# Message instructions of four steps instead of two in the first graph's edge pass

## The chip, the cores and the metric

One core of a Trainium2 chip runs the whole program. The metric is the time of one execution on the device in microseconds (us). Engines are named as in the profile: PE is TensorE (the matrix engine), PEld its weight loads, DVE is VectorE, ACT is ScalarE, POOL is GpSimd, SP is SyncE. A wait is a semaphore wait in an engine's own instruction stream: everything behind it on that engine waits too.

## The reference

Two rounds of a graph layer and a feed-forward layer on 6250 nodes of 256 features, with 106250 edges sorted by their destination. Only the attention over the edges of the first graph layer matters here:

```python
Q = (h @ Wq).reshape(n, H, HD)          # n = 6250, H = 8 heads, HD = 32
K = (h @ Wk).reshape(n, H, HD)
V = (h @ Wv).reshape(n, H, HD)
score = jnp.einsum('ehd,ehd->eh', K[src], Q[dst]) / np.sqrt(HD) + edge_bias
m = jax.ops.segment_max(score, dst, num_segments=n)
ex = jnp.exp(score - m[dst])
denom = jax.ops.segment_sum(ex, dst, num_segments=n)
attn = ex / denom[dst]
out = jax.ops.segment_sum(attn[:, :, None] * V[src], dst, num_segments=n)
```

After it come the projection, layer norms, a feed-forward layer, a feed-forward layer on the top half of the nodes, a second graph layer and a mixture of eight experts. All is float32.

## The kernel before

`attend_edges` works through the edges in steps of 128 edges, one edge per partition. A step belongs to one block of 128 destination nodes. 16 steps make a chunk (`CH`), 4 a quarter (`QU`), 2 a pair, and there are 55 chunks (`CHUNKS_OF`), 880 steps. A step goes through these stations:

- POOL gathers the key and value rows of its 128 source nodes into `ring`, 44 steps deep (L411).
- PE multiplies a one-hot matrix with the block's queries, so that each edge has its query row (`query`, L436, two steps into one bank), and DVE multiplies these with the keys (`product`, L661, 512 columns) and sums over each head (`dot`, L667, four steps).
- Per chunk DVE makes the scores (`score_of`, L674), PE transposes them (L457), and a row of scans on DVE finds each edge's segment maximum (L681 to L731), with two small detours through PE: `row` (L461 to L463), which `before` (L691) waits for, and `ends` (L467, L468), which `carry_of` (L716) waits for. ACT takes the exponential, PE transposes it back and ACT copies it into `prob` (L595).
- DVE multiplies the values with the weights into `msg` (`messages`, L753), 264 columns a step of which 32 of each 33 are messages and the 33rd is the weight itself, copied in by ACT (`denominators`, L580). `msg` has two halves of one quarter each. ACT also makes the one-hot matrices `sel` of each quarter (`one_hot`, L571 and L574).
- PE multiplies `sel` with `msg` (`add_up`, L450, into one of two banks), and DVE adds the result to the block's row in `qa` (`add`, L766). `add_up` of step i waits for the addition of step i - 2, since it has two banks; `add` of step i waits for that matmul.

Three chunks are in work at once: in a turn, c is the chunk whose products are made, a the one whose maxima are found, b the one whose messages are made and added up. The order of the instructions of a turn is written out by hand, on DVE in `turn` (L777 to L829), on PE and ACT in functions of the same name. `score_of` opens the turn on DVE. PE's order, as far as it matters here, is: transposed scores, add_up 0 and 1, a query pair and a one-hot, `row`, add_up 2 and 3, a query pair, `ends`, add_up 4, and so on to add_up 12 and 13, a query pair and one-hot of the next chunk, add_up 14, another query pair, add_up 15.

Before the change a message instruction makes one pair, 512 columns, and adds 1 to `s_msg`. PE waits for `s_msg` at every even step, for the pair of that step alone; at the first step of a quarter it also waits for the one-hot (`s_rs`) and for the denominators (`s_den`). A pair that opens a quarter waits until PE has added up the quarter two before it. ACT overwrites a half of `prob` when all messages of the chunk two back are made.

Of the kernel before, what the change touches and what calls it, by code (L numbers as in the profile page):

```python
# [16 lines left out]
ALU = mybir.AluOpType  # L17
# [3 lines left out]
P = 128  # L21
# [308 lines left out]
def attend_edges(nc, g, qa):  # L330
# [3 lines left out]
    with Phase(nc, "attend") as m:  # L334
# [81 lines left out]
        def _(pe):  # L416
# [23 lines left out]
            def add_up(b, *steps):  # L440
                for u in steps:
                    q, i = u // QU, b * CH + u
                    if u % QU == 0:
                        pe.wait_ge(s_rs, b * quarters + q + 1)
                        pe.wait_ge(s_den, b * quarters + q + 1)
                    if u % 2 == 0:
                        pe.wait_ge(s_msg, i // 2 + 1)
                    if i >= SUM_BANKS:
                        pe.wait_ge(s_add, i - SUM_BANKS + 1)
                    nc.tensor.matmul(ps_agg[i % SUM_BANKS][:, 0:AGG], sel[:, q % 2, u % QU, :], msg[:, q % 2, u % QU, :],  # L450
                                     start=True, stop=True).then_inc(s_agg, 1)
# [105 lines left out]
        def _(act):  # L557
# [33 lines left out]
            def weights_of(a):  # L591
                act.wait_ge(s_prob, a + 1)
                if a >= 2:
                    act.wait_ge(s_msg, (a - 1) * CH // 2)
# [44 lines left out]
        def _(v):  # L639
# [107 lines left out]
            def messages(b, pair):  # L747
                q, first, u = pair // 2, (b * CH + pair * 2) % RING1, pair * 2
                if pair == 0:
                    v.wait_ge(s_weights, b + 1)  # L750
                if pair % 2 == 0 and b * quarters + q >= 2:
                    v.wait_ge(s_agg, (b * quarters + q - 1) * QU)
                nc.vector.tensor_tensor(msg[:, q % 2, u % QU:u % QU + 2].rearrange("p u (h c) -> p u h c", c=HC)[:, :, :, 0:HD],  # L753
                                        ring[:, first:first + 2, D:2 * D].rearrange("p u (h d) -> p u h d", h=H),
                                        prob[:, b % 2].rearrange("p h u -> p u h")[:, u:u + 2, :].unsqueeze(3)
                                        .to_broadcast([P, 2, H, HD]), ALU.mult).then_inc(s_msg, 1)
# [20 lines left out]
            def turn(c, a, b):  # L777
# [8 lines left out]
                of(b, messages, 1)  # L786
# [6 lines left out]
                of(a, top_of)  # L793
                of(b, add, at, 2)
                of(a, drop_of)
                of(b, messages, 2)
# [4 lines left out]
                of(b, messages, 3)  # L801
# [10 lines left out]
                of(b, messages, 4)  # L812
# [4 lines left out]
                of(b, messages, 5)  # L817
# [4 lines left out]
                of(b, messages, 6)  # L822
# [3 lines left out]
                of(b, messages, 7)  # L826
# [2139 lines left out]
```

## Time and profile before

| | us |
|---|---|
| median of 3 runs | 5128.81 |
| lowest and highest | 5120.07, 5130.25 |
| the profiled execution | 5127.6 |
| its span, first to last instruction | 5125.8 |

| engine | busy us | share of the span |
|---|---|---|
| PE | 3909.5 | 76% |
| DVE | 3118.7 | 61% |
| POOL | 2344.6 | 46% |
| ACT | 1867.0 | 36% |

The pass of the change is the first of three long DVE stretches; its message instructions run from 284.5 to 1740.5 us of the span. A row of the profile gives a group of instructions by its line in the kernel, its engine and its tiles: busy us and the mean ns of one, then the engine's idle time just before them and who ended it. In a timeline the rows stand in order of time: start, duration, engine, line, count of merged instructions, and idle time before the first with its releaser. A step of `add_up` is two matmul instructions, so "x2" is one step and "x4" two. DVE durations overlap a little: the next one starts before the last has ended. PEclk is the clock that TensorE was granted, as a share of 2.4 GHz.

### The profile page before, as it was taken

To read this page: it belongs to the slowest core of one execution; us is meant where nothing else is said; L and a number is where in the kernel's file an instruction comes from. 1 tells how busy PE (TensorE), PEld (TensorE's weight loads), DVE (VectorE), ACT (ScalarE), POOL (GpSimd) and SP (SyncE) were. 2 spreads that over 40 slices of the span, in tenths; PEclk is the share of its full clock that TensorE was granted. 3 is DMA by queue.
4 is the path that set the end of the run, shared out by engine and by line. 5 is a ranking of instruction groups with operands and counts; after the bars stand their busy time and mean duration, and the time that the engine had idled before them with its cause. 6 is when DMAs were issued, how large, how long until landed. Compare 5 with 4: busy or idle time off the path is not lost. (4 is left out here: it accounts for less than half of the span.)

```text
span 5125.8 us, 69922 instructions
## 1 busy us (share of the span) xinstructions
PE 3909.5 (76%) x16154; PEld 2806.8 (55%) x16282; DVE 3118.7 (61%) x7733; ACT 1867.0 (36%) x5097; POOL 2344.6 (46%) x2387
## 2 busy tenths in 40 slices
PE   6977777777777659967965777777774349999998
PEld 3555555555555448856843444444443336777776
DVE  3389989999999766662045777777777761111111
ACT  1334444444444213311213555555553303333332
POOL 2265555556555340001045777777773402333332
PEclk8989999999999789987966778787776569999999
DMA  2565555555555232211064444444443441211111
GB/s 75 182 186 160 164 159 160 161 160 165 162 156 160 66 105 92 92 58 41 31 201 129 110 109 110 108 111 110 111 110 86 132 148 29 33 31 31 31 32 27
DMA packets 316121, 553.59 MB, mean 108 GB/s; under 512 B 63430, under 2 KB 213782, under 8 KB 315856
## 3 DMA queue, kind: packets, MB, share of 16 engines
q0 software_dynamic: 137120, 388.63, 28.9%
q1 hardware_dynamic: 178736, 161.98, 10.4%
q8 instruction: 99, 1.62, 0.1%
q14 instruction: 166, 1.36, 0.1%
HBM read 459.75 MB, written 90.62 MB: 107 GB/s over the span
## 5 line engine op out<-in xcount | busy, mean ns | idle before, releaser
L411 POOL DMA_INDIRECT attend_ring<-kv_rows,all_step_src x880 | 867.5, 986 | 592.5 <-PE attend_ps_agg L450 440.0
L914 POOL DMA_INDIRECT edge_ring<-head_rows,all_step_src x880 | 863.9, 982 | 285.2 <-issue 185.5
L950 PE MATMUL edge_ps_agg<-edge_msg,edge_sel 128*128 128x264 f32 x1760 | 644.7, 492 | 208.3 <-DVE graph_acc L1249 105.7
L450 PE MATMUL attend_ps_agg<-attend_msg,attend_sel 128*128 128x264 f32 x1760 | 591.3, 441 | 243.5 <-DVE graph_qa L766 138.1
L2799 DVE TENSOR_TENSOR moe_gl<-moe_ps_h,moe_act 128x341 f32<-128x341 f32 x210 | 107.9, 514 | 776.7 <-PE moe_ps_h L2717 776.7
L950 PEld LDWEIGHTS edge_ps_agg<-edge_msg,edge_sel 128*128 128x128 f32 x1760 | 374.9, 237 | 352.6 <-issue 171.3
L450 PEld LDWEIGHTS attend_ps_agg<-attend_msg,attend_sel 128*128 128x128 f32 x1760 | 317.7, 204 | 415.3 <-DVE graph_qa L766 182.7
L436 PE MATMUL attend_ps_q<-graph_qa,attend_sel_t 128*128 x1760 | 512.2, 419 | 7.1 <-DVE attend_prod L661 6.4
L2717 PE MATMUL moe_ps_h<-experts_w,moe_xt 128*128 x1680 | 501.8, 451 | 0.6 <-ACT moe_xt L2748 0.6
L766 DVE SCALAR_TENSOR_TENSOR graph_qa<-graph_qa,all_step_same,attend_ps_agg 128x264 f32 x880 | 421.8, 479 | 58.8 <-PE attend_ps_agg L450 42.4
L571 ACT ACTIVATE attend_sel<-all_lane,all_step_dst 128x128 f32<-128x128 f32 x880 | 281.2, 390 | 429.6 <-PE attend_ps_agg L450 414.0
L2671 POOL DMA_INDIRECT out<-moe_y,moe_to_row x105 | 166.6, 1587 | 579.9 <-ACT moe_y L2757 565.0
L436 PEld LDWEIGHTS attend_ps_q<-graph_qa,attend_sel_t 128*128 128x128 f32 x1760 | 368.6, 212 | 76.0 <-issue 11.0
L2717 PEld LDWEIGHTS moe_ps_h<-experts_w,moe_xt 128*128 128x128 f32 x1680 | 311.1, 190 | 146.5 <-issue 3.1
L1249 DVE TENSOR_TENSOR graph_acc<-graph_acc,edge_ps_agg 128x264 f32 x880 | 365.7, 416 | 30.6 <-PE edge_ps_agg L950 20.1
L1237 DVE TENSOR_TENSOR edge_msg<-edge_ring,edge_prob 128x256 f32<-128x256 f32 x880 | 345.8, 414 | 37.0 <-ACT edge_prob L1113 35.1
L1061 ACT ACTIVATE edge_sel<-all_lane,all_step_dst 128x128 f32<-128x128 f32 x880 | 279.5, 389 | 237.4 <-PE edge_ps_agg L950 237.4
L2702 PE MATMUL moe_ps_y<-experts_w,moe_gt 128*128 x1260 | 309.9, 387 | 0.7 <-ACT moe_gt L2774 0.7
L661 DVE TENSOR_TENSOR attend_prod<-attend_ps_q,attend_ring 128x512 f32<-128x512 f32 x440 | 297.8, 678 | 20.3 <-DMA attend_ring<-kv_rows,all_step_src 10.1
L753 DVE TENSOR_TENSOR attend_msg<-attend_ring,attend_prob 128x512 f32<-128x512 f32 x440 | 298.9, 679 | 0.3 <-issue 0.2
L1808 PE MATMUL ffn_ps_h<-ffn_xt,ffn_wa 128*128 128x256 f32 x1216 | 272.0, 382 | 11.5 <-ACT ffn_xt L1831 11.5
L1850 ACT ACTIVATE ffn_ht<-ffn_ps_h,ffn_ba 128x256 f32<-128x256 f32 x304 | 144.2, 474 | 363.9 <-PE ffn_ps_h L1808 363.9
(423 smaller groups left out, 6374.8 us busy)
## 6 DMA issues: line engine op xcount, KB each, us to landing
attend_ring<-kv_rows,all_step_src POOLq DMA_INDIRECT x880
edge_ring<-head_rows,all_step_src POOLq DMA_INDIRECT x880
kv_rows<-qkv_kv SPq DMA_DIRECT2D x25, 512.0 KB, 2.9
experts_w<-in_w_t SPq DMA_DIRECT2D x16, 682.0 KB
attend_mask<-run_starts SPq DMA_DIRECT2D x440, 8.1 KB
edge_mask<-run_starts SPq DMA_DIRECT2D x440, 8.1 KB
head_rows<-hds_hh SPq DMA_DIRECT2D x25, 264.0 KB, 3.4
qkv_x<-in_x SPq DMA_DIRECT2D x25, 256.0 KB, 3.3
```

The source lines that it names most:

```text
L411: nc.gpsimd.indirect_dma_start(ring[:, step % RING1, :], None, g.kv_rows, bass.IndirectOffsetOnAxis(g.step_src[:, step:step + 1], 0)).then ...
L436: ins = nc.tensor.matmul(ps_q[k % QBANKS][:, i, :], sel_t[:, q % 2, u % QU, :], queries[:, bass.ds(blocks[u % U], 1), :].rearrange("p b d ...
L450: nc.tensor.matmul(ps_agg[i % SUM_BANKS][:, 0:AGG], sel[:, q % 2, u % QU, :], msg[:, q % 2, u % QU, :], start=True, stop=True).then_inc(s_ ...
L661: nc.vector.tensor_tensor(prod[:, at:at + 2, :], ps_q[k % QBANKS][:], ring[:, first:first + 2, 0:D], ALU.mult).then_inc(s_prod, 1)
L753: nc.vector.tensor_tensor(msg[:, q % 2, u % QU:u % QU + 2].rearrange("p u (h c) -> p u h c", c=HC)[:, :, :, 0:HD], ring[:, first:first + 2 ...
L766: nc.vector.scalar_tensor_tensor(at[u % U], at[u % U], g.step_same[:, i:i + 1], ps_agg[i % SUM_BANKS][:, 0:AGG], ALU.mult, ALU.add).then_i ...
L914: nc.gpsimd.indirect_dma_start(ring[:, n % slots, u, :], None, g.head_rows, bass.IndirectOffsetOnAxis(g.step_src[:, step:step + 1], 0)).th ...
L950: nc.tensor.matmul(ps_agg[i % BANKS][:, 0:AGG], sel[:, q % 2, u % QU, :], msg[:, q % 2, u % QU, :], start=True, stop=True).then_inc(s_agg, 1)
L1237: nc.vector.tensor_tensor(msg[:, q % 2, u % QU].rearrange("p (h c) -> p h c", c=HC)[:, :, 0:HD], ring[:, b % slots, u, 0:D].rearrange("p ( ...
L1249: nc.vector.tensor_tensor(at[u % U], at[u % U], ps_agg[i % BANKS][:, 0:AGG], ALU.add).then_inc(s_add, 1)
L2702: last = nc.tensor.matmul(ps_y[:], gt[0:size, c, :], w2[0:size, :, c, :][:, bass.ds(e, 1), :].rearrange("p a d -> p (a d)"), start=(c == 0 ...
L2717: last = nc.tensor.matmul(ps_h[2 * i + hf][:, 0:EHALF], xt[:, slot, k, :], w13[:, :, k, i, hf * EHALF:(hf + 1) * EHALF][:, bass.ds(e, 1), ...
```

## The change

`messages` makes a whole quarter in one instruction of 1024 columns, four in a chunk, and adds 1 to `s_msg` for each. In DVE's order the four stand where pairs 0 and 4 stood (quarters 0 and 2), between the top row and the addition of step 2 (quarter 1), and where pair 6 stood (quarter 3). PE waits at every step for the quarter of that step. Every quarter's instruction waits for the release of its half of `msg`. ACT's wait counts quarters instead of pairs.

```diff
@@ -443,8 +443,7 @@
                     if u % QU == 0:
                         pe.wait_ge(s_rs, b * quarters + q + 1)
                         pe.wait_ge(s_den, b * quarters + q + 1)
-                    if u % 2 == 0:
-                        pe.wait_ge(s_msg, i // 2 + 1)
+                        pe.wait_ge(s_msg, b * quarters + q + 1)
                     if i >= SUM_BANKS:
                         pe.wait_ge(s_add, i - SUM_BANKS + 1)
                     nc.tensor.matmul(ps_agg[i % SUM_BANKS][:, 0:AGG], sel[:, q % 2, u % QU, :], msg[:, q % 2, u % QU, :],
@@ -591,7 +590,7 @@
             def weights_of(a):
                 act.wait_ge(s_prob, a + 1)
                 if a >= 2:
-                    act.wait_ge(s_msg, (a - 1) * CH // 2)
+                    act.wait_ge(s_msg, (a - 1) * quarters)
                 nc.scalar.activation(prob[:, a % 2].rearrange("p h u -> p (h u)"), prob_e, ACT.Copy).then_inc(s_weights, 1)
 
             for s in range(2):
@@ -744,16 +743,16 @@
                 nc.vector.scalar_tensor_tensor(heads_at, shrinks.unsqueeze(2).to_broadcast([P, H, HC]), 1.0, heads_at,
                                                ALU.add, ALU.mult).then_inc(s_v, 1)
 
-            def messages(b, pair):
-                q, first, u = pair // 2, (b * CH + pair * 2) % RING1, pair * 2
-                if pair == 0:
+            def messages(b, q):
+                first, u = (b * CH + q * QU) % RING1, q * QU
+                if q == 0:
                     v.wait_ge(s_weights, b + 1)
-                if pair % 2 == 0 and b * quarters + q >= 2:
+                if b * quarters + q >= 2:
                     v.wait_ge(s_agg, (b * quarters + q - 1) * QU)
-                nc.vector.tensor_tensor(msg[:, q % 2, u % QU:u % QU + 2].rearrange("p u (h c) -> p u h c", c=HC)[:, :, :, 0:HD],
-                                        ring[:, first:first + 2, D:2 * D].rearrange("p u (h d) -> p u h d", h=H),
-                                        prob[:, b % 2].rearrange("p h u -> p u h")[:, u:u + 2, :].unsqueeze(3)
-                                        .to_broadcast([P, 2, H, HD]), ALU.mult).then_inc(s_msg, 1)
+                nc.vector.tensor_tensor(msg[:, q % 2].rearrange("p u (h c) -> p u h c", c=HC)[:, :, :, 0:HD],
+                                        ring[:, first:first + QU, D:2 * D].rearrange("p u (h d) -> p u h d", h=H),
+                                        prob[:, b % 2].rearrange("p h u -> p u h")[:, u:u + QU, :].unsqueeze(3)
+                                        .to_broadcast([P, QU, H, HD]), ALU.mult).then_inc(s_msg, 1)
 
             def add(b, at, *steps):
                 for u in steps:
@@ -783,7 +782,6 @@
                 of(c, product, 1)
                 of(a, heads_of)
                 of(b, rescale, at[0])
-                of(b, messages, 1)
                 of(b, add, at, 0)
                 of(a, before)
                 of(a, row_forward)
@@ -791,14 +789,13 @@
                 of(a, row_backward)
                 of(b, add, at, 1)
                 of(a, top_of)
+                of(b, messages, 1)
                 of(b, add, at, 2)
                 of(a, drop_of)
-                of(b, messages, 2)
                 of(a, after)
                 of(b, add, at, 3)
                 of(c, product, 2)
                 of(a, carry_of)
-                of(b, messages, 3)
                 of(a, forward)
                 of(b, add, at, 4)
                 of(c, product, 3)
@@ -809,21 +806,19 @@
                 of(b, add, at, 6)
                 of(a, shrink_of)
                 of(c, product, 4)
-                of(b, messages, 4)
+                of(b, messages, 2)
                 of(b, add, at, 7)
                 of(c, product, 5)
                 at = rows_of(b, 1) if b is not None else [None] * U
                 of(b, add, at, 8)
-                of(b, messages, 5)
                 of(c, dot, 2)
                 of(b, add, at, 9)
                 of(c, product, 6)
                 of(b, add, at, 10)
-                of(b, messages, 6)
+                of(b, messages, 3)
                 of(b, add, at, 11)
                 of(c, product, 7)
                 of(b, add, at, 12)
-                of(b, messages, 7)
                 of(b, add, at, 13)
                 of(c, dot, 3)
                 of(b, add, at, 14, 15)
```

## Rows read from the trace of the kernel before

**Rows 1.** Busy time: window, its length, PE, PEld, DVE, ACT, POOL, PEclk, DMA, GB/s.

```profile
300.00:1700.00 1400.00, 1053.69 (x4170) 762.75 (x4239) 1284.15 (x2672) 580.64 (x1625) 821.00 (x832) 0.93 0.57 160
954.26:979.53 25.27, 18.49 (x80) 13.12 (x81) 24.33 (x51) 11.08 (x32) 16.12 (x17) 1.00 0.60 171
1006.05:1032.36 26.31, 19.82 (x79) 14.48 (x81) 24.63 (x52) 11.08 (x32) 15.84 (x17) 0.94 0.58 164
1032.36:1060.56 28.20, 21.37 (x80) 15.31 (x81) 24.41 (x52) 11.07 (x32) 15.64 (x17) 0.88 0.54 152
1060.56:1088.36 27.80, 21.47 (x80) 15.63 (x81) 24.78 (x52) 11.07 (x32) 16.29 (x17) 0.88 0.58 160
```

**Rows 2.** Groups of instructions on VectorE, from 300 to 1700 us.

```profile
L753 DVE TENSOR_TENSOR attend_msg<-attend_ring,attend_prob 128x512 f32<-128x512 f32 x420 | 285.3, 679 | 0.1
...
L667 DVE TENSOR_REDUCE attend_dots<-attend_prod 128x32 f32<-128x1024 f32 x211 | 253.9, 1203 | 0.0
```

**Rows 3.** All score instructions (L674): shortest, median, longest ns, first and last start.

```profile
L674 DVE SCALAR_TENSOR_TENSOR attend_score<-attend_dots,all_step_bias x55: 373/375/381, 264.9 to 1702.5; 128x128 f32<-128x128 f32 x55
```

**Rows 4.** Waits from 300 to 1700 us: total us, times, the longest.

```profile
PE attend_ps_agg L450 <- DVE graph_qa L766: 135.5, 108, 2.1
...
PE attend_ps_agg L450 <- DVE attend_msg L753: 58.4, 54, 1.1
...
PE attend_ps_agg L450 <- ACT attend_msg L580: 29.7, 52, 0.6
```

**Rows 5.** The page's costliest groups: messages of the second graph's pass.

```profile
L1237 DVE TENSOR_TENSOR edge_msg<-edge_ring,edge_prob 128x256 f32<-128x256 f32 x880 | 345.8, 414 | 37.0 <-ACT edge_prob L1113 35.1
```

**Rows 6.** Timeline of VectorE in the chunk from 954.26 to 979.53.

```profile
954.48 0.67 DVE L753 TENSOR_TENSOR attend_msg<-attend_ring,attend_prob 128x512 f32<-128x512 f32 x1
955.07 0.69 DVE L661 TENSOR_TENSOR attend_prod<-attend_ps_q,attend_ring 128x512 f32<-128x512 f32 x1
...
958.38 0.16 DVE L691 COPY attend_ps_tp<-attend_so_far 1x8 f32<-1x8 f32 x1
958.57 0.41 DVE L695 TENSOR_TENSOR_SCAN attend_c_in<-attend_keep,attend_ps_tp 1x128 f32<-1x128 f32 x1
...
968.43 0.67 DVE L753 TENSOR_TENSOR attend_msg<-attend_ring,attend_prob 128x512 f32<-128x512 f32 x1
...
970.59 0.68 DVE L753 TENSOR_TENSOR attend_msg<-attend_ring,attend_prob 128x512 f32<-128x512 f32 x1
...
973.71 0.68 DVE L753 TENSOR_TENSOR attend_msg<-attend_ring,attend_prob 128x512 f32<-128x512 f32 x1
...
975.48 0.49 DVE L766 SCALAR_TENSOR_TENSOR graph_qa<-graph_qa,all_step_same,attend_ps_agg 128x264 f32 x1
975.89 0.69 DVE L753 TENSOR_TENSOR attend_msg<-attend_ring,attend_prob 128x512 f32<-128x512 f32 x1
...
978.79 0.49 DVE L766 SCALAR_TENSOR_TENSOR graph_qa<-graph_qa,all_step_same,attend_ps_agg 128x264 f32 x1 [0.30 <-PE attend_ps_agg L450]
```

**Rows 7.** Timeline of TensorE in the same chunk.

```profile
955.60 1.13 PE L450 MATMUL attend_ps_agg<-attend_msg,attend_sel 128*128 128x264 f32 x4 [0.58 <-ACT attend_msg L580]
...
958.07 0.27 PE L463 MATMUL attend_ps_tp<-all_ident,attend_runs 128*1 128x128 f32 x1
...
969.35 1.13 PE L450 MATMUL attend_ps_agg<-attend_msg,attend_sel 128*128 128x264 f32 x4
...
972.85 0.71 PE L450 MATMUL attend_ps_agg<-attend_msg,attend_sel 128*128 128x264 f32 x2 [0.81 <-DVE graph_qa L766]
...
974.65 1.13 PE L450 MATMUL attend_ps_agg<-attend_msg,attend_sel 128*128 128x264 f32 x4 [1.08 <-DVE attend_msg L753]
...
976.70 0.64 PE L450 MATMUL attend_ps_agg<-attend_msg,attend_sel 128*128 128x264 f32 x2
...
978.04 0.61 PE L450 MATMUL attend_ps_agg<-attend_msg,attend_sel 128*128 128x264 f32 x2
```

**Rows 8.** Timeline of ScalarE in the same chunk.

```profile
955.25 0.40 ACT L580 ACTIVATE attend_msg<-attend_prob 128x32 f32<-128x32 f32 x2
```

## The prediction

> **What bounds the kernel now.** The change touches only the attention pass over the edges of the first graph, so I read only that stretch. First the busy time of its steady part: VectorE (DVE) works 1284 of 1400 us, 92%, TensorE (PE) 1054 us, 75% [rows 1]. VectorE is the engine nearest its limit, and the message instructions are a large item on it: 420 of 679 ns in that stretch, eight to a chunk [rows 2]. The pass has 55 chunks of 16 steps; their score instructions start 26.62 us apart on average ((1702.5 - 264.9) / 54) [rows 3].
>
> Then who waits for whom. TensorE waits for VectorE's additions 108 times (135.5 us) and for the messages 54 times (58.4 us, up to 1.1), and 52 times, 0.57 us each, for ScalarE's denominators [rows 4]. That is about once per chunk at fixed places, so the loop is not VectorE alone: it is VectorE and TensorE handing work to each other, and the places must be looked at one by one.
>
> Last, one chunk in order of time: the one from 954.26 to 979.53, whose TensorE clock was 1.00 (2.4 GHz) all through, so that nothing but the waits sets its 25.27 us [rows 1]. The other chunks shown take 26.31 to 28.20 at a mean granted clock of 0.94 to 0.88. Steps of a chunk are numbered 0 to 15, pairs 0 to 7, quarters 0 to 3.
>
> **The price of the new instruction.** 256 columns take 414 ns in the second graph's pass [rows 5], 512 take 679 [rows 2]: 1.035 ns a column. 1024 columns then take 1.21 us; the reduction that reads 1024 columns takes 1.203 [rows 2]. VectorE starts the next instruction before the last has ended: pair 0 starts at 954.48, its follower at 955.07, 0.59 later [rows 6]. With 0.53 for 512 more columns the new one holds the engine 1.13. Two old ones hold it 1.20: a quarter saves 0.07 us, 220 quarters 15 us. If the new one took as long as two (1.36 us) nothing would be saved; I take 1.21, the nearer rows.
>
> The Trainium skill ("VectorE: DVE Perf Modes", the section on the fixed extra latency of SBUF-source operations) charges each fp32 tensor_tensor (N + 151) / 0.96 ns. Its durations agree with the 679 above; read as time of the engine it would save 157 ns a quarter, 35 us in all. The 0.59 us from start to start speaks against that reading.
>
> **Quarter 0, start of the chunk.** TensorE's step 0 starts at 955.60 [rows 7]. Its messages (pair 0) ended at 955.15; the last thing it waited for was the denominators, the first of two ScalarE copies from 955.25, which end at 955.50 and 955.65 [rows 8]. With one instruction for four steps the messages end at 954.48 + 1.21 = 955.69 and take the place of that wait. How long from there to the matmul? Step 12 is released by pair 6, which ends at 974.39, and starts at 974.65: 0.26. So step 0 starts at 955.95, **0.35 later**. What is queued behind it on TensorE is steps 0 and 1, a query pair, a one-hot and the row transposes, back to back until 958.34; VectorE's L691 waits for these and starts at 958.38 [rows 6, 7]. It goes to 958.73. VectorE has pair 1's 0.60 fewer and quarter 0's 0.53 more before it, so it arrives early and stands idle: its saving ends there.
>
> **Quarter 1.** It moves from before step 0's addition (and pair 2 and 3 from after the drop and the carry) to the place after the top row. From L691 to the second dot product two pairs of 0.60 go and one of 1.13 comes, -0.07; small dependent instructions that the pairs covered are bare now, 0.19 each as from L691 to L695 [rows 6]; the gap of the top row is covered instead. I put the sum at -0.03. Step 4 has its messages long before. The shift is **0.32**. In chunks at the low clock VectorE waits for the carries of TensorE there instead, which carry the same 0.35.
>
> **Quarter 2.** Pair 4 started at 968.43 and ended at 969.10; step 8 started at 969.35 [rows 6, 7]. The new one ends at 968.43 + 0.32 + 1.21 = 969.96, step 8 starts at 970.21, 0.86 later, and a query pair and steps 9 and 10 are queued behind. But TensorE stood idle 0.81 before step 11, at 972.85, for step 9's addition [rows 7]. That slack takes it: the addition comes by VectorE's own shift, 0.32 + 1.13 - 2 x 0.60 = **0.25**, since pair 5 (970.59) is gone too.
>
> **Quarter 3.** It starts at 973.71 + 0.25 = 973.96 and ends at 975.17, where pair 6 ended at 974.39. TensorE stood idle 1.08 for exactly this [rows 7]. With the same 0.26, step 12 starts at 975.43, **0.78 later** than 974.65. Behind it are steps 12 and 13, the next chunk's first queries, step 14, more queries and step 15, without a wait to 978.04. Pair 7 (975.89) ended at 976.58, when TensorE was just ready for step 14, at 976.70: its removal frees nothing on TensorE. On VectorE it frees 0.60, after step 12's addition (975.48, now 976.26), but the addition of step 15, which stood idle 0.30 for TensorE and started at 978.79, then only waits longer [rows 6, 7]. The next score follows it. So the chunk ends 0.77 later.
>
> **Nothing else is on the path.** The extra semaphore wait at every odd step is passed before the wait for the addition that follows it, in TensorE's queue, hidden by the matmuls still running: at 0; bare, it could cost no more than the 0.12 us between release and matmul at step 14. ScalarE waits only for chunks two back. The gathers on the GpSimd queue are released by the same steps, a little later, with POOL busy 821 of 1400 us. SyncE's row loads are released by the same scores. Nothing of them is moved. On VectorE quarters 2 and 3 wait for the half of the buffer that steps 0 to 3 and 4 to 7 used; both stand behind additions of later steps, so these waits are met.
>
> **Sum.** 54 chunk periods x 0.77 = 41.6 us. The granted clock adds a little: 26.62 less 25.27 is 1.35 us a chunk, and if the low stretches keep their share of a period 3% longer, 2 us more. The profiled execution took 5127.6 us (span 5125.8), 1.2 under the median of the three runs, 5128.8: with 42 to 44 added to either, 5171.
>
> Bounds. If TensorE starts 0.12 behind its messages, as at step 14 (976.58 and 976.70), both waits are 0.14 shorter: 0.49 a chunk, 5155. If the instruction takes 1.36: about 0.15 more a chunk, 5179.
>
> **The rivals.**
> A. VectorE is the bound after all: for it, 92%; against it, the 1.08 and 0.30 of idle time at the chunk's end. It decides if TensorE reaches step 12 later than the messages even when these take 1.21. Then the kernel gains 15 us, 5114; and if the engine's time falls by the difference of durations, 2 x 0.679 - 1.21 = 0.15 a quarter, 33 us, 5096. Chance 0.09.
> B. Gain and waits cancel, the same time within 0.2% (10 us, about what a measurement of this kernel can tell from no change): 0.11.
> C. Only quarter 3 costs: TensorE makes up the 0.35 before L691 (a step 0 released by the denominators as before). 0.42 a chunk, 23 us, 5151: 0.15.
> D. The waits are as forecast and TensorE's clock falls more often. Low stretches are there already: a chunk whose mean granted clock is 0.94 costs 1.04 more than one at 1.00, one at 0.88 2.5 to 2.9 more [rows 1]. TensorE's idle time grows by 0.35 at the start of a chunk and 0.5 before step 12. One more low stretch in every fourth chunk at 1.5 us is 20 us: 5191. Chance 0.15; one less, 5151, lies within the range.
>
> The Trainium skill has a rule for either side in one section ("Perfetto Trace Analysis", Optimizing Scalar/DVE Operations): grouping helps where the engine is saturated, and where it is not but makes bubbles on others, breaking instructions up helps. The 1.08 us of idle TensorE puts this pass under the second, by which the change is the wrong way round.
>
> **How the numbers follow.** Forecast 0.50 (own range 5155 to 5182), D 0.15, C 0.15: slower 0.80. The range from 5138 to 5200 holds these and the upper edge of B. Likeliest 5171.
>
> **What the profile would show.** 220 message instructions of 1.21 us with the next start 1.13 behind; step 0 released by the messages and no more by the denominators; TensorE idle about 1.6 before step 12; VectorE idle about 0.5 before L691; a chunk at full clock of 26.0 us. It is wrong if a full-clock chunk takes 25.2 or less, or if the wait before step 12 stays near 1.1.

## The result and the profile after

| | before | after |
|---|---|---|
| median of the runs, us | 5127.49 (6 runs) | 5154.33 (6 runs) |
| lowest and highest | 5120.07, 5130.25 | 5142.99, 5158.44 |
| ratio, 95% interval | | 1.0052 (1.0039 to 1.0065) |
| the profiled execution | 5127.6 | 5150.87 |
| its span | 5125.8 | 5149.1 |

The changed kernel is slower by 0.5%, 27 us. The forecast was 5171, 42 us slower, range 5138 to 5200. In the whole document a program's time is the median of all its executions and a ratio is taken from the fast ones alone, which leaves out one execution of 5570.89 us in e3, one of 12549.58 in e7 and one of 9381.73 of the kernel before on the chip of e7.

The change did what it says. One row of the groups of instructions of the changed kernel, VectorE, 300 to 1700 us (its lines stand one or a few lower: `messages` is L752, `add_up` L449, `add` L765, the score L673, `before` L690, its transpose L462):

```profile
L752 DVE TENSOR_TENSOR attend_msg<-attend_ring,attend_prob 128x1024 f32<-128x1024 f32 x206 | 248.9, 1208 | 0.0
```

1.208 us for 1024 columns; 1.21 was taken. The score instructions of the pass:

```profile
L673 DVE SCALAR_TENSOR_TENSOR attend_score<-attend_dots,all_step_bias x55: 372/375/382, 264.1 to 1731.1; 128x128 f32<-128x128 f32 x55
```

(1731.1 - 264.1) / 54 = 27.17 us a chunk, where [rows 3] gave 26.62: 0.54 more, 29 us over the pass. The rest of the program took 6 us less in this execution, so the span grew by 23. The kernel before was profiled once, and that profile is the one that all later ones are compared with.

Busy time, the steady part and two chunks (window, length, PE, PEld, DVE, ACT, POOL, PEclk, DMA, GB/s):

```profile
300.00:1700.00 1400.00, 1008.30 (x4087) 753.54 (x4154) 1265.91 (x2411) 569.44 (x1594) 831.45 (x824) 0.93 0.55 158
1077.06:1104.14 27.08, 19.65 (x80) 14.65 (x81) 24.70 (x48) 11.07 (x32) 16.12 (x17) 0.94 0.54 157
1048.60:1077.06 28.46, 20.79 (x80) 15.52 (x81) 24.77 (x47) 11.06 (x32) 16.10 (x17) 0.88 0.53 152
```

The mean granted clock of the steady part is 0.93 as in [rows 1]. But no chunk of the pass ran at 1.00 all through any more. 42 of the 50 inner chunks (the 54 periods without the first two and the last two) are like the second row here: a clock of 0.94, one low stretch that starts 7 to 8 us behind the score, 27.08 us. In the kernel before the chunks of that kind take 26.31 [rows 1].

Waits of the same stretch (total us, times, longest):

```profile
PE attend_ps_agg L449 <- DVE attend_msg L752: 156.0, 154, 1.7
...
PE attend_ps_agg L449 <- DVE graph_qa L765: 114.9, 76, 2.2
...
DVE attend_ps_tp L690 <- PE attend_ps_tp L462: 26.5, 51, 1.8
```

In [rows 4] TensorE waited 54 times for the messages, now 154 times: at steps 0, 8 and 12 of each chunk. The 52 waits for ScalarE's denominators are gone. VectorE's L690 now waits in every chunk.

The two timelines of the chunk from 1077.06, first VectorE, then TensorE:

```profile
1077.28 1.21 DVE L752 TENSOR_TENSOR attend_msg<-attend_ring,attend_prob 128x1024 f32<-128x1024 f32 x1
1078.41 0.68 DVE L660 TENSOR_TENSOR attend_prod<-attend_ps_q,attend_ring 128x512 f32<-128x512 f32 x1
...
1081.52 0.16 DVE L690 COPY attend_ps_tp<-attend_so_far 1x8 f32<-1x8 f32 x1 [0.27 <-PE attend_ps_tp L462]
...
1092.61 1.20 DVE L752 TENSOR_TENSOR attend_msg<-attend_ring,attend_prob 128x1024 f32<-128x1024 f32 x1
...
1097.82 1.22 DVE L752 TENSOR_TENSOR attend_msg<-attend_ring,attend_prob 128x1024 f32<-128x1024 f32 x1
...
1100.12 0.49 DVE L765 SCALAR_TENSOR_TENSOR graph_qa<-graph_qa,all_step_same,attend_ps_agg 128x264 f32 x1
...
1103.40 0.49 DVE L765 SCALAR_TENSOR_TENSOR graph_qa<-graph_qa,all_step_same,attend_ps_agg 128x264 f32 x1 [0.56 <-PE attend_ps_agg L449]
1104.14 0.38 DVE L673 SCALAR_TENSOR_TENSOR attend_score<-attend_dots,all_step_bias 128x128 f32<-128x128 f32 x1 [0.25 <-issue]
```

```profile
1078.74 1.13 PE L449 MATMUL attend_ps_agg<-attend_msg,attend_sel 128*128 128x264 f32 x4 [0.92 <-DVE attend_msg L752]
...
1081.21 0.27 PE L462 MATMUL attend_ps_tp<-all_ident,attend_runs 128*1 128x128 f32 x1
...
1094.06 1.13 PE L449 MATMUL attend_ps_agg<-attend_msg,attend_sel 128*128 128x264 f32 x4 [0.42 <-DVE attend_msg L752]
...
1096.96 0.71 PE L449 MATMUL attend_ps_agg<-attend_msg,attend_sel 128*128 128x264 f32 x2 [0.46 <-DVE graph_qa L765]
1099.29 1.13 PE L449 MATMUL attend_ps_agg<-attend_msg,attend_sel 128*128 128x264 f32 x4 [1.62 <-DVE attend_msg L752]
...
1102.64 0.61 PE L449 MATMUL attend_ps_agg<-attend_msg,attend_sel 128*128 128x264 f32 x2
```

These answer to [rows 6, 7]. The quarter's instruction starts at 1077.28 and its follower at 1078.41, 1.13 later. Step 0 starts at 1078.74, 1.68 behind the score (1.34 before). L690 stands idle 0.27 for the transpose ("about 0.5" was forecast) and starts 4.46 behind the score (4.12 before). TensorE is idle 0.42 before step 8, 0.46 before step 11 (0.81 before) and 1.62 before step 12 (1.08 before). The addition of step 15 waits 0.56 for it, where [rows 6] had 0.30.

### The profile page after: what moved, and what is told of

Its sections match the earlier page's. It is cut to its first block and busy times, and to the rows that moved or that the text cites. A ratio compares the mean times of both kernels' runs of the same rounds, so it can differ in the third digit from the quotient of the medians.

```text
span 5149.1 us, 69482 instructions
## 1 busy us (share of the span) xinstructions
PE 3896.3 (76%) x16154; PEld 2821.2 (55%) x16282; DVE 3126.5 (61%) x7513; ACT 1866.0 (36%) x5097; POOL 2361.4 (46%) x2387
## 3 DMA queue, kind: packets, MB, share of 16 engines
q14 instruction: 164, 1.34, 0.1%
## 5 line engine op out<-in xcount | busy, mean ns | idle before, releaser
L411 POOL DMA_INDIRECT attend_ring<-kv_rows,all_step_src x880 | 886.1, 1007 | 602.8 <-PE attend_ps_agg L449 444.1
L449 PE MATMUL attend_ps_agg<-attend_msg,attend_sel 128*128 128x264 f32 x1760 | 576.5, 433 | 303.6 <-DVE attend_msg L752 164.8
L449 PEld LDWEIGHTS attend_ps_agg<-attend_msg,attend_sel 128*128 128x128 f32 x1760 | 322.5, 203 | 447.5 <-issue 188.7
L765 DVE SCALAR_TENSOR_TENSOR graph_qa<-graph_qa,all_step_same,attend_ps_agg 128x264 f32 x880 | 423.5, 481 | 90.7 <-PE attend_ps_agg L449 61.0
L1814 PE MATMUL ffn_ps_y<-ffn_wb,ffn_ht 128*128 128x256 f32 x1216 | 268.7, 379 | 0.0
```

The lines of the kernel that those rows point to most:

```text
L411: nc.gpsimd.indirect_dma_start(ring[:, step % RING1, :], None, g.kv_rows, bass.IndirectOffsetOnAxis(g.step_src[:, step:step + 1], 0)).then ...
L765: nc.vector.scalar_tensor_tensor(at[u % U], at[u % U], g.step_same[:, i:i + 1], ps_agg[i % SUM_BANKS][:, 0:AGG], ALU.mult, ALU.add).then_i ...
```

## A correction to what stands ahead

The section on the change, and the prediction, say that TensorE waits for `s_msg` at every step. The new line stands under the condition for a quarter's first step, so it waits once a quarter, and the "extra wait at every odd step" does not exist. It was costed at 0 and nothing hangs on it.

## How the experiments are read

A chunk is compared with chunks of its own kind: those at full clock, and those with one low stretch that starts about 7 to 8 us behind the score (mean clock 0.94). The price of a wait is the difference between these. The time of the program has the mix of kinds in it as well.

In the kernels of the experiments the table `MSGS` lists the message instructions of a chunk, each with its first step and its number of steps, and `MSG_OF` says which of them each pair belongs to. TensorE waits at every even step for the instruction that holds it. The code cuts show this table and the calls in VectorE's `turn` that are new; later calls are renumbered.

| kernel | program, us | ratio to before (95%) | mean period | at full clock | one low stretch |
|---|---|---|---|---|---|
| before | 5127 | 1 | 26.62 | 25.27 | 26.31 |
| changed | 5154 | 1.0052 (1.0039 to 1.0065) | 27.17 | none | 27.08 |
| quarter 3 in pairs (e6) | 5151 | 1.0050 (1.0037 to 1.0064) | 27.14 | none | 26.64 |
| quarter 0 in pairs (e7) | 5152 | 1.0051 (1.0038 to 1.0064) | 27.19 | none | 26.74 |
| quarters 0 and 3 in pairs (e5) | 5101 | 0.9949 (0.9935 to 0.9962) | 26.26 | 25.29 | 26.30 |
| before, 2 fillers | 5102 | 0.9953 (0.9939 to 0.9966) | 26.31 | 25.28 | none |
| changed, 2 fillers | 5149 | 1.0039 (1.0025 to 1.0052) | 27.17 | 26.07 | none |
| quarters 1 and 2 merged, 2 fillers | 5100 | 0.9952 (0.9938 to 0.9965) | 26.30 | 25.29 | none |
| before, 3 fillers | 5043 | 0.9837 (0.9824 to 0.9850) | 25.20 | 25.28 | none |
| changed, 3 fillers | 5088 | 0.9924 (0.9911 to 0.9937) | 26.03 | 26.07 | none |

The last two columns are medians over such inner chunks, taken from the starts of the score instructions. A ratio is to the kernel before on the same chip.

## Experiments, first batch: which quarter costs

The chip of this batch was another: the kernel before itself took 5497.93 us there (11 runs). So its program times say little; its traces still show where each instruction stands in a chunk.

**e1, quarter 3 in pairs.**

```diff
+    MSGS, MSG_OF = ((0, 4), (4, 4), (8, 4), (12, 2), (14, 2)), (0, 0, 1, 1, 2, 2, 3, 4)
...
                 of(b, add, at, 12)
+                of(b, messages, 4)
                 of(b, add, at, 13)
```

> The changed kernel with quarter 3 back in two pairs at their old places; quarters 0 to 2 stay one instruction each. Theory (two waits of TensorE, one at step 0, one at step 12, make the loss): the wait before step 12 falls back from about 1.6 us to near 1.1, and a chunk with one low-clock stretch takes 26.31 + 0.25 = 26.56 us, where the kernel before has 26.31 and the changed one 27.08. That is 0.52 less than the changed kernel: about 28 us less over 54 chunks if the clock stays as it is, so the program within 15 us of the kernel before. Rival (the long instructions cost by themselves or by their places, wherever they stand): three quarters of the loss stay, about 20 us over the kernel before, 26.9 us a chunk.

Measured: 5542.40 us, ratio 1.0078 (1.0033 to 1.0122). The addition of step 12 came 22.46 us into a chunk with one low stretch; in the kernel before it comes at 22.25 and in the changed one at 23.06. So up to there the forecast holds (+0.21), and TensorE's idle time before step 12 is 1.08 again. Behind it nearly every chunk of this chip stood still for another 2 us and more before the addition of step 15, and the period could not be read.

**e2, quarter 0 in pairs.**

```diff
+    MSGS, MSG_OF = ((0, 2), (2, 2), (4, 4), (8, 4), (12, 4)), (0, 1, 2, 2, 3, 3, 4, 4)
...
                 of(b, rescale, at[0])
+                of(b, messages, 1)
                 of(b, add, at, 0)
```

> The changed kernel with quarter 0 back in two pairs at their old places; quarters 1 to 3 stay one instruction each. Theory: step 0 is released by ScalarE's denominators again, L691's counterpart starts 0.35 us earlier than in the changed kernel, and of the 0.77 us a chunk the 0.42 of quarter 3 stay: 26.73 us a chunk with one low-clock stretch. Program about 23 us over the kernel before, less what the clock gives. Rival (only quarter 3 costs, step 0's delay is made up before the row of VectorE that waits): nothing changes against the changed kernel, 27.08 us.

Measured: 5493.86 us, ratio 0.9998 (0.9982 to 1.0015). L692, the counterpart of `before`, starts 4.12 us into a chunk as in the kernel before, so the 0.34 are gone. The one chunk with a low stretch of the usual place that the chip left undisturbed took 26.74 us. The disturbance is this row of the waits ("remote" is a releaser on another engine, seen only by its semaphore):

```profile
DVE graph_qa L768 <- remote: 59.8, 25, 2.8
```

The kernel before has no such row in [rows 4]'s stretch on its own chip. Its cause stays open.

**e3, only quarters 1 and 2 merged.** Both edits together, six message instructions a chunk.

> Only quarters 1 and 2 are one instruction each, quarters 0 and 3 stay pairs as before. Theory: neither of TensorE's two waits grows, and what VectorE saves from start to start counts: 26.31 - 0.10 to 0.15 = about 26.2 us a chunk, the program 5 to 8 us under the kernel before, if the clock is the same. Rival (moving quarter 1 behind the top row costs something itself): 26.4 us or more, the program slower than before.

Measured: 5513.95 us, ratio 1.0022 (0.9981 to 1.0063): inconclusive (the executions lie between 5482.93 and 5570.89). It was run again, as e5.

**e4, the places without the size.**

```diff
                 of(b, messages, 0)
+                of(b, messages, 1)
...
-                of(b, messages, 1)
+                of(b, messages, 2)
+                of(b, messages, 3)
...
-                of(b, messages, 2)
+                of(b, messages, 4)
+                of(b, messages, 5)
...
-                of(b, messages, 3)
+                of(b, messages, 6)
+                of(b, messages, 7)
```

> Eight pair instructions as before, but two and two together at the four places of the changed kernel; TensorE waits for each pair. VectorE saves nothing here. Theory (what costs is that the first steps of a quarter wait for all four): step 0 and step 12 start as in the kernel before, the wait before step 12 is near 1.1 us; only the additions queued behind the second pair come 0.6 us later, which can cost step 13 up to 0.28. A chunk with one low-clock stretch takes 26.3 to 26.6 us. Rival (the places are what costs, not the size of the instruction): 27.1 us or more, since VectorE has 0.28 us a chunk more to do than in the changed kernel.

Measured: 5507.54 us, ratio 1.0009 (0.9989 to 1.0028). VectorE's timeline of one chunk (score at 1489.45), then TensorE's; "x2" in L755 is two pairs:

```profile
1489.67 1.27 DVE L755 TENSOR_TENSOR attend_msg<-attend_ring,attend_prob 128x512 f32<-128x512 f32 x2
...
1509.82 1.27 DVE L755 TENSOR_TENSOR attend_msg<-attend_ring,attend_prob 128x512 f32<-128x512 f32 x2
...
1517.49 0.49 DVE L768 SCALAR_TENSOR_TENSOR graph_qa<-graph_qa,all_step_same,attend_ps_agg 128x264 f32 x1 [2.41 <-remote]
```

```profile
1490.78 1.13 PE L451 MATMUL attend_ps_agg<-attend_msg,attend_sel 128*128 128x264 f32 x4 [0.57 <-ACT attend_msg L581]
...
1510.75 1.52 PE L451 MATMUL attend_ps_agg<-attend_msg,attend_sel 128*128 128x264 f32 x4 [1.08 <-issue]
...
1514.49 0.61 PE L451 MATMUL attend_ps_agg<-attend_msg,attend_sel 128*128 128x264 f32 x2
```

Step 0 starts 1.33 behind the score, idle for ScalarE's denominators, and step 12 is idle 1.08: both as in the kernel before, though the instructions stand where the changed kernel has them. Four chunks of this run have no low stretch before step 12; in the one whose score is at 751.02, TensorE starts step 12 20.36 behind the score, where the kernel before at full clock has 20.39 (974.65 - 954.26 in [rows 1, 7]):

```profile
771.38 1.65 PE L451 MATMUL attend_ps_agg<-attend_msg,attend_sel 128*128 128x264 f32 x4 [1.08 <-DVE attend_msg L755]
```

So it is the size of the instruction, the time until the first steps of a quarter may start, that makes the two waits, and not the places; up to step 12 the places cost nothing. What they cost behind it, and so the chunk's length that the theory and the rival forecast, isn't settled: step 15's matmuls start at 1514.49 in the profile and its addition at 1517.49, 2.41 us of it idle. That is the disturbance of this chip, and the kernel was not run again.

## Second batch: the clock

The runs of this batch are from one chip and those of the third batch from another; the kernel before takes 5126.12 us on the first and 5125.11 on the second.

The fillers are matmuls that nobody reads, put where TensorE idles:

```diff
-        ps_c = m.ps("ps_c", [P, 32])
+        ps_c = m.ps("ps_c", [P, 512])
...
+            def warm(times):
+                for _ in range(times):
+                    nc.tensor.matmul(ps_c[:, 64:64 + 448], g.ident[:], g.step_bias[:, 0:448], start=True, stop=True)
...
-                    add_up(b, 2, 3)
+                    add_up(b, 2)
+                    warm(1)
+                    add_up(b, 3)
...
                     add_up(b, 10, 11)
+                    warm(1)
```

> The kernel before with two filler matmuls a chunk on TensorE (a constant times the identity, 448 float32 columns, into unused columns of a PSUM bank; nothing reads them), placed where TensorE idles for VectorE: behind step 2 (1.71 us of idle time) and behind step 11. Theory (in the kernel before, the low-clock stretches come from these idle times, and cost 26.62 - 25.27 = 1.35 us a chunk on average): nearly all low stretches go, nearly every chunk takes 25.27 us, and the pass is up to 73 us shorter. Rival (the fillers are not enough, or stand in the way): the low stretches stay, the mean period stays at 26.6 us or grows.

Measured: 5102.13 us, ratio 0.9953 (0.9939 to 0.9966), 24 us faster. Steady part, and a chunk at full clock:

```profile
300.00:1700.00 1400.00, 1117.23 (x4493) 763.29 (x4492) 1289.66 (x2707) 587.77 (x1648) 838.69 (x833) 0.95 0.57 160
974.35:999.63 25.28, 20.10 (x85) 13.88 (x85) 24.34 (x51) 11.07 (x32) 16.13 (x17) 1.00 0.61 170
```

The clock rises from 0.93 to 0.95. 13 of 50 chunks take 25.28 us. But the 37 others each have one low stretch of another place (it starts 1.3 to 2.7 us behind the score), and the mean period fell by 0.31 and not by 1.35. Half right: the idle times were the cause of the stretches that went, and the fillers were too few.

> The changed kernel with the same two fillers. Theory (the two waits cost 0.77 us a chunk at equal clock, and in the plain kernels the clock gave 0.23 of it back, since the changed kernel has 3.75 us of low clock a chunk instead of 4.03): at full clock all through, a chunk takes 26.04 us, and the difference between the two kernels with fillers is 0.77 x 54 = 42 us, where it is 29 in the pass without fillers. Rival (0.54 us is the true price of the waits, and the like-for-like 0.77 is chance): 29 us between the two.

Measured: 5148.76 us, ratio 1.0039 (1.0025 to 1.0052):

```profile
300.00:1700.00 1400.00, 1073.69 (x4362) 753.53 (x4361) 1252.49 (x2410) 569.37 (x1593) 837.54 (x825) 0.95 0.56 158
1103.96:1130.03 26.07, 19.83 (x85) 14.05 (x85) 24.39 (x47) 11.07 (x32) 16.21 (x17) 1.00 0.59 164
```

26.07 us at full clock against 25.28, **0.79**; 0.77 was forecast for this. Between the two kernels with fillers lie 46.6 us, not 29. The theory's 42 is the nearer.

> Only quarters 1 and 2 as one instruction, with the same two fillers. Theory: at full clock a chunk takes 25.1 to 25.2 us, 4 to 8 us less over the pass than the kernel before with fillers: the fastest of all. Rival (moving quarter 1 behind the top row costs what the merging saves): the same as the kernel before with fillers.

Measured: 5100.21 us, ratio 0.9952 (0.9938 to 0.9965), 25.29 us at full clock: the same as the kernel before with fillers (5102.13 and 25.28). The rival holds in its number. Its reason, that moving quarter 1 eats the saving, is not what the trace shows; e5, which has the same order, answers it below.

> The same kernel as e3_q12_only, on what may be another chip: there the additions of step 15 waited 1.6 us and more for TensorE in most chunks, which the kernel before does not show in its own trace, so the comparison was unclear. In the few undisturbed chunks with one low-clock stretch the period was 26.28 us against 26.31. Theory: same or up to 5 us faster than the kernel before. Rival: slower by 10 us or more, as the median there had it.

Measured: 5101.03 us, ratio 0.9949 (0.9935 to 0.9962), 25 us **faster** than before. Neither theory had that. The steady part and two chunks:

```profile
300.00:1700.00 1400.00, 1051.10 (x4273) 756.34 (x4271) 1301.91 (x2597) 586.81 (x1645) 837.72 (x832) 0.94 0.57 160
1023.30:1048.59 25.29, 18.52 (x81) 13.21 (x81) 24.43 (x49) 11.07 (x32) 16.02 (x16) 1.00 0.60 169
968.97:995.27 26.30, 19.95 (x81) 14.58 (x81) 24.63 (x50) 11.06 (x32) 16.13 (x16) 0.94 0.58 165
```

At equal clock the chunk is as long as it was: 25.29 against 25.27, 26.30 against 26.31. Yet a part of the saving was there. TensorE in the chunk at 1023.30, then VectorE in it, then VectorE in the kernel before, behind the pair at 975.89 in [rows 6]:

```profile
1043.65 1.13 PE L451 MATMUL attend_ps_agg<-attend_msg,attend_sel 128*128 128x264 f32 x4 [1.08 <-DVE attend_msg L755]
```

```profile
1044.88 0.75 DVE L755 TENSOR_TENSOR attend_msg<-attend_ring,attend_prob 128x512 f32<-128x512 f32 x1
1045.55 0.48 DVE L768 SCALAR_TENSOR_TENSOR graph_qa<-graph_qa,all_step_same,attend_ps_agg 128x264 f32 x1
```

```profile
976.49 0.48 DVE L766 SCALAR_TENSOR_TENSOR graph_qa<-graph_qa,all_step_same,attend_ps_agg 128x264 f32 x1
```

TensorE starts step 12 20.35 behind the score, where it was 20.39: 0.04 earlier, and in the chunks with one low stretch 0.08 (medians 21.35 and 21.43). Then pair 7's instruction takes 0.75 us and the next addition starts 0.67 behind it, where the kernel before has 0.69 and 0.60. It is so in 44 of the 50 inner chunks here and in none of the kernel before. In these 44 the time from the start of step 12 to the next score is 4.95 us; in the 6 others it is 4.89, and in the kernel before 4.88 (medians). So 0.06 is lost together with pair 7's longer instruction, and that eats the saving; the moved quarter 1 cost nothing up to step 12. Step 14's matmuls, which start just behind pair 7's messages, are 0.06 longer in the same 44 chunks. Which of the two holds up the other, and why, no run shows.

What changed for the program is the mix: 17 of 50 inner chunks at full clock instead of 8, and a clock of 0.94 instead of 0.93. The pass is 19 us shorter (0.36 a chunk), and that comes from where TensorE's low stretches fell and not from the work: with two fillers the same two kernels lie 2 us apart (5102.13 and 5100.21). The profiled spans differ by 26; the other 7 us lie behind the pass, where the two programs do the same, and stay unexplained.

## Third batch: the clock taken out, and the two quarters alone

The third filler stands on TensorE behind `add_up` 15:

```diff
                     add_up(b, 15)
                 if a is not None:
+                    warm(1)
                     at_node(a)
```

> The kernel before with a third filler matmul a chunk, behind step 15, ahead of the 1.2 us in which TensorE waits for the next score. With two fillers the low-clock stretch from 7 us and the one from 21 us of a chunk were gone, and one that starts 1.3 to 2.5 us after the score was left in three chunks of four (2.53 us of low clock a chunk, mean period 26.31). Theory: it comes from the idle time around the score; with the third filler nearly all chunks run at full clock in 25.27 us, the pass takes 1.35 us x 54 = 73 us less than in the plain kernel, the program about 5055. Rival (low stretches come anyway, or the filler delays the weights of the rescaling): mean period 26 us or more.

Measured: 5043.05 us, ratio 0.9837 (0.9824 to 0.9850): **82 us faster than the kernel before**, and the fastest of all. Steady part and a chunk; then its score instructions; then the three fillers in TensorE's timeline:

```profile
300.00:1700.00 1400.00, 1137.78 (x4717) 776.57 (x4716) 1327.04 (x2783) 599.18 (x1676) 860.96 (x853) 0.99 0.58 162
968.76:994.04 25.28, 20.85 (x87) 14.26 (x87) 24.33 (x51) 11.07 (x32) 16.12 (x17) 1.00 0.61 170
```

```profile
L683 DVE SCALAR_TENSOR_TENSOR attend_score<-attend_dots,all_step_bias x55: 372/375/379, 266.0 to 1626.7; 128x128 f32<-128x128 f32 x55
```

```profile
973.48 0.92 PE L456 MATMUL attend_ps_c<-all_step_bias,all_ident 128*128 128x448 f32 x2
...
987.91 0.91 PE L456 MATMUL attend_ps_c<-all_step_bias,all_ident 128*128 128x448 f32 x2
...
992.99 0.92 PE L456 MATMUL attend_ps_c<-all_step_bias,all_ident 128*128 128x448 f32 x2
```

All 50 inner chunks are at 1.00 (the 0.99 is the end of the window, behind the pass). The mean period is (1626.7 - 266.0) / 54 = 25.20. The clock had cost 26.62 - 25.20 = 1.42 us a chunk, 77 us; that is the pass, and the other 5 us of the 82 lie outside of it. Each filler takes 0.9 us of TensorE and delays nothing: a chunk at full clock is 25.28 us long with them and 25.27 without.

The Trainium skill ("Perfetto Trace Analysis", Matmul Optimizations) says that the matmul engine scales its power with its utilization, so that matmuls should run back to back. The rows above agree: matmuls of no use, in the gaps, brought the clock to 1.00.

> The changed kernel with the three fillers. Theory (0.77 to 0.79 us a chunk at full clock, whatever the clock does in the plain kernels): nearly all chunks take 26.06 us, 42 us more over the pass than the kernel before with three fillers. Rival (TensorE's longer waits still make it fall to the low clock): low stretches stay here where they are gone in the other, and the difference is 60 us or more.

Measured: 5088.43 us, ratio 0.9924 (0.9911 to 0.9937):

```profile
300.00:1700.00 1400.00, 1101.11 (x4623) 767.68 (x4624) 1301.60 (x2509) 594.11 (x1666) 843.79 (x832) 1.00 0.58 160
910.08:936.15 26.07, 20.58 (x87) 14.43 (x87) 24.39 (x47) 11.08 (x32) 16.18 (x17) 1.00 0.60 165
```

```profile
L683 DVE SCALAR_TENSOR_TENSOR attend_score<-attend_dots,all_step_bias x55: 373/375/389, 263.4 to 1668.9; 128x128 f32<-128x128 f32 x55
```

26.07 us a chunk at full clock; mean (1668.9 - 263.4) / 54 = 26.03. The pass is 1405.5 us long against 1360.7: **45 us** for the change with the clock taken out, and 45.4 between the programs. 42 was forecast for this pair. Of the 3 us above it, 1.6 are one inner chunk that still has a low stretch and takes 27.71 us, and 1 is 0.79 in place of 0.77 in each chunk. The rival's "60 or more" falls.

> The same kernel as e1_q3_pairs (quarter 3 in pairs, the rest as changed), because its first chip stalled TensorE behind step 15. There step 12's addition came at 22.46 us of a chunk with one low stretch, against 22.25 before and 23.06 changed. Theory: on an undisturbed chip the chunk takes 26.31 + 0.22 to 0.25 = 26.55 us with one low stretch and 25.5 at full clock. Rival: 26.9 or more. The program's time follows this and the share of low clock, which moved the kernel with quarters 1 and 2 merged by 25 us without a change of the chunk at equal clock; so the program may lie anywhere from 5105 to 5150.

Measured: 5150.96 us, ratio 1.0050 (1.0037 to 1.0064). Steady part and a chunk, then TensorE's steps 0 and 12 in it:

```profile
300.00:1700.00 1400.00, 1043.45 (x4159) 761.80 (x4158) 1267.85 (x2464) 569.57 (x1594) 830.83 (x826) 0.91 0.57 158
939.75:966.39 26.64, 19.86 (x81) 14.55 (x81) 24.74 (x49) 11.07 (x32) 16.13 (x16) 0.94 0.59 161
```

```profile
941.43 1.13 PE L451 MATMUL attend_ps_agg<-attend_msg,attend_sel 128*128 128x264 f32 x4 [0.92 <-DVE attend_msg L755]
...
961.45 1.13 PE L451 MATMUL attend_ps_agg<-attend_msg,attend_sel 128*128 128x264 f32 x4 [1.08 <-DVE attend_msg L755]
```

Step 0 is 1.68 behind the score as in the changed kernel, step 12 idle for 1.08 as in the kernel before. The chunk takes 26.64, +0.33, where +0.25 was forecast. TensorE starts step 12 21.70 behind the score, 0.27 later than the 21.43 of the kernel before, close to the 0.25; the other 0.06 comes with pair 7's longer instruction, as in e5 (43 of 50 chunks have it).

> The same kernel as e2_q0_pairs (quarter 0 in pairs, the rest as changed). In the one undisturbed chunk with one low stretch on the first chip it took 26.74 us. Theory: 26.73 to 26.75 with one low stretch, 25.7 at full clock; the price of quarter 3 alone, 0.43. Rival (quarter 0's delay is made up elsewhere): 27.08 as in the changed kernel. The program from 5120 to 5160, by the share of low clock.

Measured: 5152.04 us, ratio 1.0051 (1.0038 to 1.0064):

```profile
300.00:1700.00 1400.00, 1034.44 (x4154) 751.88 (x4152) 1260.28 (x2461) 568.76 (x1593) 830.67 (x823) 0.93 0.57 158
1104.98:1131.72 26.74, 19.85 (x81) 14.66 (x81) 24.68 (x48) 11.07 (x32) 16.12 (x17) 0.94 0.58 162
```

```profile
1106.32 1.13 PE L451 MATMUL attend_ps_agg<-attend_msg,attend_sel 128*128 128x264 f32 x4 [0.58 <-ACT attend_msg L581]
...
1126.88 1.13 PE L451 MATMUL attend_ps_agg<-attend_msg,attend_sel 128*128 128x264 f32 x4 [1.62 <-DVE attend_msg L755]
```

Step 0 is released by the denominators again, 1.34 behind the score, and step 12 is idle for 1.62. The chunk takes 26.74, +0.43; forecast +0.42.

The two add up: 0.33 + 0.43 = 0.76, against 0.77 for both together (quarters 1 and 2 are merged in all of these, which by e5 costs a chunk nothing). Yet each of them alone costs the program as much as both: 26, 27 and 27 us against the kernel before on the same chip. In e6 the clock goes with it: 0.91 over the steady part. In e7 it reads 0.93 as in the changed kernel, and only the count of the chunks tells: 20 of 50 take 26.74, and 23 take 27.4, with the low stretch at the end of the chunk, where 42 of the changed kernel's have the cheaper one.

## Why the prediction was right, and where not

- **The price of the instruction** (1.21 us, next start 1.13 later): 1.208 and 1.13. The reading of the Trainium skill's formula as time of the engine, by which a merged quarter saves 157 ns, falls as the prediction had it: from start to start it saves 0.07, and of that nothing reached the end of a chunk (e5).
- **Quarter 0**: step 0 forecast 0.35 later, measured 0.34; L691's counterpart 0.35, measured 0.34. The time from the end of the messages to the matmul, taken as 0.26, was 0.25 at steps 0 and 12. By itself 0.34 of a chunk (27.08 - 26.74).
- **Quarters 1 and 2**: shifts of -0.03 and -0.07 were forecast, and the 0.81 of slack before step 11 was to take quarter 2. TensorE's idle time before step 11 fell from 0.81 to 0.46 and took it. With these two quarters alone TensorE started step 12 0.04 to 0.08 earlier, but behind it 0.06 was lost where pair 7's instruction was longer, and the chunk stayed at 25.29 for 25.27 (e5). The prediction had no such term; with all four quarters merged there is no pair 7.
- **Quarter 3**: wait before step 12 forecast "about 1.6", measured 1.62; with this quarter alone a chunk grew by 0.43. In the changed kernel TensorE starts step 12 22.23 behind the score for 21.43 (with one low stretch), 0.80 later; 0.78 was forecast.
- **Sum at equal clock**: forecast 0.77, measured 0.77 (one low stretch) and 0.79 (full clock).
- **The step that failed is the clock's term.** The prediction let the low stretches keep their share of a period and added 2 us. They did not: against its own run without low stretches, the kernel before loses 26.62 - 25.20 = 1.42 us a chunk to them and the changed one 27.17 - 26.03 = 1.14. That gives 0.28 x 54 = 15 us back, and 45 - 15 = 30 is what the pass grew by (29). Rival D looked at the same term with the other sign: the changed kernel's inner chunks have 3.75 us of low clock each, the kernel before's 4.02, and only 5 of the 50 have a second stretch, where 17 of the kernel before's have. The measured 5154 lies at the lower edge of the forecast's own range (5155 to 5182), which had been set for another reason, a release in 0.12 us, that did not come. So the stated range held the time with the waits as forecast and the clock not.
- **The upper bound is added up wrong.** If the instruction took 1.36 us, 0.15 more, both waits would grow by that, since quarter 0's delay is carried into quarter 3: 0.30 more a chunk and 5187, not 0.15 and 5179. The range, up to 5200, holds it all the same.
- **Rival C gave 5151**, nearer the measured 5154 than the forecast, by a mechanism that isn't there: e7 shows that quarter 0 costs its 0.34. A time alone would have confirmed it.
- **Rival A** (VectorE is the bound) falls: with four message instructions that each hold VectorE 0.07 us less than two pairs, the changed kernel's chunk is 0.77 longer. The Trainium skill's rule on breaking instructions up, that the prediction set against the change, is borne out for steps 0 and 12 by e4: two instructions in the same place bring both waits back to what they were.

Left open: why the low stretches fall as they do in each kernel. That they follow TensorE's idle time is shown by the fillers; which chunk gets one was only counted. Open too is why pair 7's instruction and step 14 grow by 0.06 us in e5 and e6.

## What to carry to other kernels

In a loop where two engines hand work to each other, an instruction's size has two prices: the engine's time, and how late the first consumer may start. Look at which wait of the consumer the producer ends last, and keep the small instruction there; merge only where the consumer has slack, and expect little from it. When a change is worth less than the spread of the TensorE clock, compare stretches of equal granted clock, or take the clock out with filler matmuls, before believing the program's time; here the fillers were worth three times the change itself.

## What was not expected of the hardware

- A change that leaves a chunk as long as it was at equal clock (e5) made the program 25 us faster, and prices of 0.33, 0.43 and 0.77 us a chunk all came out as 26 to 27 us. Where the low stretches fall is worth as much as the change.
- Three unread matmuls a chunk, 0.9 us each, brought the pass to 1.00 and gave 82 us, 77 of them in the pass.
- The same message instruction on 512 columns, in the same place, took 0.69 us in one kernel and 0.75 in another (pair 7 in e5).
- The same program took 5498 us on one chip and 5126 on others, with waits of VectorE for step 15 of a chunk (59.8 us in e2 from 300 to 1700 us) that are missing elsewhere. They are not the whole of it: in e2's profile the pass is 130 us longer than in the kernel before's, and the rest of the program 241.
